# The first radial layer of two neighbouring edge groups on two row groups of PE, issued behind each other

## The chip, the cores and the metric

The kernel runs on one NeuronCore of a Trainium2 chip. The metric is the device time of one execution in microseconds (us), as the median of several runs.

## What is computed

A layer of a graph network: 6250 nodes with 160 channels (64 scalars and 32 vectors of three), 206250 edges sorted by their destination node.

```python
h = jnp.maximum(_layernorm(x, axis=-1), 0.0)
# per node: l0, l1 = linear maps of h times node_attr (the table that is gathered); si0, si1 likewise
h = jax.nn.relu(edge_length_embedded @ W_fc1 * (1.0 / np.sqrt(N_BASIS))) * RELU_GAIN   # 10 -> 100 per edge
w = h @ W_fc2 * (1.0 / np.sqrt(N_RADIAL))                                             # 100 -> 192 per edge
y0 = l0[edge_src]
y1 = l1[edge_src]
m0 = w0 * y0 * e0
m1 = (w1 * y0)[:, :, None] * e1[:, None, :]
m2 = (w2 * e0)[:, :, None] * y1
m3 = w3 * jnp.einsum('eud,ed->eu', y1, e1) * INV_SQRT3
s0 = jax.ops.segment_sum(m0, edge_dst, num_segments=N) * inv    # and s1, s2, s3
out = x + si + 0.5 * (the sums through four last linear maps)
```

## The kernel before

**The node stage.** The first part normalizes the nodes, applies the linear map and stores the result as a table in HBM. It ends before the first gather of the edge phase, and the change leaves it as it is.

**The edge phase.** The edges are taken in tiles of 128, four tiles (T) to a group, four groups (G) to a turn. A pair is two turns, that is 8 groups. There are 403 groups that hold edges. For each group:

- SP loads, once for two groups (HALF), the 10 radial numbers of each edge (`rad`), the source indices (`idx`) and the edge attributes (`attr_sb`), line 272, 277 and 281, into one of two buffers c. SP's queue is in order, and the three loads of a half wait for `fc1_done`, for `gathered` and for `msg_done`.
- GpSimd (POOL) issues four indirect DMAs (L357), each of which gathers 128 rows of the table into `y`. `y` has four slots, so the gathers of group g wait for the messages (`msg_done`) of group g - 4. There are 1612 of them, and GpSimd does nothing else in this phase.
- TensorE (PE) does the first radial layer `fc1` (L867: w_fc1 against `rad`, a contraction over 10 rows, 512 columns) into the bank s = g % 2 of `ps_h`.
- ScalarE (ACT) takes the relu of it into `hr` (L462).
- PE does the second layer `fc2` (L874, four products of 192 columns) into `ps_w`.
- VectorE (DVE) builds the one-hot matrices `hot` (L672, L679) and the dot products (L645, L649), multiplies `ps_w` with `y` into `msg` (L655, L660, L665), and adds the sums of the group before to `acc` (L707).
- PE sums the messages by node: `windows` (L902 with 128 columns and L904 with 64, four tiles each).

PE's instructions are in the order in which they are written out. In every step it does `fc1(g)`, `fc2(g - 1)`, `windows(g - 2)`. Every 8 groups the loop also finishes one block of 128 nodes: ACT normalizes it, PE turns it (`turn_block`, L880 and L881, into bank 1 of `ps_h`), ACT copies it (`move_block`, L467 and L468, which raises `hidt_done`), and PE ends it with six products (`last_linear`, L886 to L892). There are 47 such blocks in the loop. A further path, `general`, serves inputs whose edges are not sorted and doesn't run here.

## Time and profile before

| what | value |
|---|---|
| time, median of 3 runs | 2146.74 us (2144.57 to 2149.59) |
| span of the one profiled execution, which is its own time | 2932.2 us |
| PE busy in it | 2451.9 us (84%) |
| PE weight loads busy | 1929.8 us (66%) |
| DVE busy | 1690.4 us (58%) |
| ACT busy | 367.2 us (13%) |
| POOL busy | 1620.7 us (55%) |
| mean granted clock of PE | 0.776 of full speed |

### The profile page before, as it was taken

The page shows a single profiled execution, that of the slowest core. Times are in us where ns is not written, and L with a number is a line of the kernel's source. Part 1 is how long each engine was busy: PE and PEld are TensorE (multiplying, and loading weights), DVE is VectorE, ACT ScalarE, POOL GpSimd, SP SyncE. Part 2 cuts the span into 40 slices and gives each one's busy share as a digit, 9 for nine tenths or more (in the row PEclk, how much of TensorE's full clock was granted, in tenths as well). Part 3 has the DMA queues.
Part 4 walks back from the last instruction along what each step waited for, and adds up shares of the span by engine and source line. Part 5 has one row for each costly group of instructions (what it writes and reads, how often), then busy time and mean ns, then how long its engine had stood idle before and what let it go on. Part 6 is the DMA issues. An engine that isn't in the chain of part 4 may idle for free.

```text
span 2932.2 us, 42148 instructions
## 1 busy us (share of the span) xinstructions
PE 2451.9 (84%) x11361; PEld 1929.8 (66%) x11361; DVE 1690.4 (58%) x4677; ACT 367.2 (13%) x818; POOL 1620.7 (55%) x1629
## 2 busy tenths in 40 slices
PE   4688878888888888888889888888888888788988
PEld 3566666676666766666667666666676666676766
DVE  7355656555555655655655655555555556565655
ACT  4200101111111110111111111111111011111111
POOL 3455555555555656555555555555655555655653
PEclk9677877776877877887876878777878778778777
DMA  3222222222222222222222222122222222222222
GB/s 106 66 49 52 53 51 50 50 53 48 53 47 51 55 49 55 50 51 53 51 72 53 53 51 52 47 49 51 55 47 54 49 49 53 54 53 51 56 51 66
DMA packets 159836, 158.31 MB, mean 54 GB/s; under 512 B 86658, under 2 KB 131750, under 8 KB 159818
## 3 DMA queue, kind: packets, MB, share of 16 engines
q0 software_dynamic: 77376, 132.16, 18.3%
q1 hardware_dynamic: 81400, 24.49, 3.7%
q10 hardware_dynamic: 1042, 1.46, 0.2%
q8 instruction: 7, 0.11, 0.0%
q14 instruction: 11, 0.09, 0.0%
HBM read 149.94 MB, written 8.03 MB: 54 GB/s over the span
## 4 chain that ended last, share of the span: by engine, by line
PE 56%; another core or an unknown queue 16%; DVE 12%; issue 10%; DVEq 3%; ACT 1%; DMA 0%; ACTq 0%; SPq 0%
PE ps_w L874 17%; PE ps_s L902 13%; PE ps_h L867 11%; PE ps_s L904 11%; DVE hot L679 2%; DVE acc L707 2%; DVEq L710 2%; DVE dot L649 2%; DVE dots L645 2%; DVE hot L672 1%; DVE msg L665 1%; PE ps_s L890 1%; PE ps_s L891 1%; PE ps_s L886 1%
## 5 line engine op out<-in xcount | busy, mean ns | idle before, releaser
L357 POOL DMA_INDIRECT y<-table,idx x1612 | 1592.2, 988 | 1283.1 <-DVE msg L665 682.1
L874 PEld LDWEIGHTS ps_w<-w_fc,hr 100*128 100x128 f32 x3224 | 662.8, 235 | 464.2 <-issue 396.3
L874 PE MATMUL ps_w<-w_fc,hr 100*128 100x192 f32 x3224 | 814.9, 407 | 61.5 <-ACT hr L462 40.9
L707 DVE TENSOR_TENSOR acc<-acc,ps_s 64x32 f32 (+1 forms) x1612 | 327.3, 203 | 759.2 <-remote 480.6
L902 PE MATMUL ps_s<-hot,msg 128*128 128x128 f32 x3224 | 590.4, 336 | 95.1 <-issue 43.1
L902 PEld LDWEIGHTS ps_s<-hot,msg 128*128 128x128 f32 x3224 | 546.8, 245 | 140.0 <-DVE msg L665 62.4
L867 PE MATMUL ps_h<-rad,w_fc 10*100 10x512 f32 x806 | 547.7, 763 | 104.7 <-ACT hid_z L468 77.4
L904 PE MATMUL ps_s<-hot,msg 128*128 128x64 f32 x3224 | 512.3, 304 | 117.0 <-issue 116.5
L904 PEld LDWEIGHTS ps_s<-hot,msg 128*128 128x128 f32 x3224 | 499.0, 230 | 120.8 <-issue 119.8
L462 ACT ACTIVATE hr<-ps_h 100x512 f32<-100x512 f32 x403 | 238.7, 597 | 2433.7 <-remote 1026.9
L655 DVE TENSOR_TENSOR msg<-ps_w,y 128x512 f32<-128x512 f32 x403 | 278.7, 692 | 316.1 <-remote 172.3
L679 DVE TENSOR_TENSOR hot<-hot,attr_sb 128x512 f32<-128x512 f32 x403 | 276.0, 685 | 0.0
L649 DVE TENSOR_REDUCE dot<-dots 128x128 f32<-128x384 f32 x403 | 236.0, 586 | 0.0
L645 DVE TENSOR_TENSOR dots<-y,attr_sb 128x384 f32<-128x384 f32 x403 | 222.4, 552 | 9.6 <-DMA y<-table,idx 9.6
L660 DVE TENSOR_TENSOR msg<-ps_w,y 128x384 f32<-128x384 f32 x403 | 220.7, 548 | 0.0
L867 PEld LDWEIGHTS ps_h<-rad,w_fc 10*100 10x100 f32 x806 | 117.6, 186 | 151.1 <-ACT hid_z L468 82.8
L672 DVE TENSOR_TENSOR hot<-iota_w,dst_rel 128x128 f32<-128x128 f32 x403 | 118.1, 293 | 20.4 <-DMA attr_sb<-in_attr 5.1
L665 DVE TENSOR_TENSOR msg<-ps_w,dot 128x128 f32<-128x128 f32 x403 | 113.3, 281 | 0.0
L692 DVE SCALAR_TENSOR_TENSOR xres<-ps_s,a_sb,xres 128x160 f32 x47 | 17.8, 378 | 106.4 <-remote 77.9
L822 PE MATMUL ps_w<-wl,hid_t 128*128 128x128 f32 x98 | 30.4, 409 | 21.2 <-DVE y L546 20.7
L418 ACT ACTIVATE hid<-xres,shift,rstd 128x128 f32 (+1 forms) x98 | 47.6, 486 | 3.6 <-DVE shift L539 3.5
L886 PE MATMUL ps_s<-w_out,fin_in 128*128 128x160 f32 x94 | 27.0, 374 | 23.3 <-DVE msg L665 16.6
(83 smaller groups left out, 556.0 us busy)
## 6 DMA issues: line engine op xcount, KB each, us to landing
y<-table,idx POOLq DMA_INDIRECT x1612
rad<-in_radial SPq DMA_DIRECT2D x202, 40.0 KB
xres<-in_x SPq DMA_DIRECT2D x7, 560.0 KB, 4.1
table<-y SPq DMA_DIRECT2D x6, 560.0 KB, 3.2
out<-xres SPq DMA_DIRECT2D x6, 560.0 KB
idx<-in_src SPq DMA_DIRECT2D x202, 4.0 KB
attr_sb<-in_attr SPq DMA_DIRECT2D x202, 16.0 KB
dst_i<-in_dst ACTq DMA_DIRECT2D x1, 808.0 KB, 6.1
```

The costliest lines, as they stand in the source:

```text
L357: nc.gpsimd.indirect_dma_start(out=y[:, j, t, :], out_offset=None, in_=table, in_offset=bass.IndirectOffsetOnAxis(ap=idx[:, j // HALF, col ...
L462: nc.scalar.activation(hr[:, s, :], ps_h[0:N_RADIAL, s, 0:GE], ACT.Relu, scale=K_RADIAL).then_inc(relu_done, 1)
L645: nc.vector.tensor_tensor(dots[:, :, :, :], vectors(j), attr_of(j, 1, 4).unsqueeze(3).to_broadcast([P, T, 3, MUL1]), ALU.mult).then_inc(do ...
L649: nc.vector.tensor_reduce(dot[:, :, :], dots[:, :, :, :].rearrange("p t d u -> p t u d"), AX.X, ALU.add).then_inc(dot_done, 1)
L655: nc.vector.tensor_tensor(msg[:, s, :, 0:2 * MUL0].rearrange("p t (k u) -> p t k u", k=2), ps_w[:, s, :, 0:2 * MUL0].rearrange("p t (k u) ...
L660: nc.vector.tensor_tensor(msg[:, s, :, 2 * MUL0:M - MUL1].rearrange("p t (d u) -> p t d u", d=3), ps_w[:, s, :, 2 * MUL0:NW - MUL1].unsque ...
L679: nc.vector.tensor_tensor(hot[:, s, :, 1:V, :], hot[:, s, :, 0:1, :].to_broadcast([P, T, 4, W]), attr_of(j, 0, 4).unsqueeze(3).to_broadcas ...
L707: nc.vector.tensor_tensor(to, to, p[rows, cols].rearrange("p (v n) -> p v n", n=W), ALU.add).then_inc(acc_done, 1)
L867: nc.tensor.matmul(ps_h[0:N_RADIAL, j % 2, 0:GE], w_fc1[:, :], rad[:, j // HALF, (j % HALF) * GE:(j % HALF + 1) * GE], start=True, stop=Tr ...
L874: ins = nc.tensor.matmul(ps_w[:, s, t, 0:NW], hr[:, s, t * P:(t + 1) * P], w_fc2[:, :], start=True, stop=True)
L902: nc.tensor.matmul(ps_s[:, s, 0:4 * W], msg[:, s, t, 0:P], hot[:, s, t, 1:V, :], start=(t == 0), stop=(t == T - 1))
L904: ins = nc.tensor.matmul(ps_s[:, s, 4 * W:6 * W], msg[:, s, t, P:M], hot[:, s, t, 0:2, :], start=(t == 0), stop=(t == T - 1))
```

## The change

`w_fc1` and `rad` are laid out twice on partitions: the first group of a half on partitions 0 to 9, the second on partitions 32 to 41 (ROW = 32). `fc1_both` issues the first layers of two neighbouring groups behind each other, one on each of the two row groups of PE, into the two banks of `ps_h`. Then PE does for the first of the two groups `windows(g - 2)` and `fc2(g)`, and for the second `windows(g - 1)` and `fc2(g + 1)`. SP issues two loads of `rad` where it issued one, each with half of the bytes. ACT issues one more load of `w_fc1` at the start. The block's `turn_block` comes after the fc2 of the fourth group of a pair, `move_block` on ACT moves one relu later, and the wait for `hidt_done` stands ahead of the next `fc1_both`. At the end PE computes the first layer of one group that holds no edges, so that 404 first layers are issued instead of 403.

```diff
--- before.py
+++ after.py
@@ -27,6 +27,7 @@
 V = 5
 G = 4
 HALF = 2
+ROW = 32
 TURNS = -(-E // (P * T * G))
 GROUPS = TURNS * G
 TILES = GROUPS * T
@@ -90,7 +91,7 @@
         wlz = sb("wlz", [P, P])
         wself = sb("wself", [P, P])
         wselfz = sb("wselfz", [MUL1, MUL1])
-        w_fc1 = sb("w_fc1", [N_BASIS, N_RADIAL])
+        w_fc1 = sb("w_fc1", [ROW + N_BASIS, N_RADIAL])
         w_fc2 = sb("w_fc2", [N_RADIAL, NW])
         w_out = sb("w_out", [P, 4, C])
         stats = sb("stats", [P, CHUNK, 6])
@@ -106,7 +107,7 @@
         hid_z = sb("hid_z", [P, 2, P])
         idx = sb("idx", [P, 2, HALF * T], I32)
         attr_sb = sb("attr_sb", [P, 2, HALF * T, 4])
-        rad = sb("rad", [N_BASIS, 2, HALF * GE])
+        rad = sb("rad", [ROW + N_BASIS, 2, GE])
         y = sb("y", [P, G, T, C])
         hr = sb("hr", [N_RADIAL, 2, GE])
         msg = sb("msg", [P, 2, T, M])
@@ -269,7 +270,8 @@
                 if not first:
                     sp.wait_ge(fc1_done, (k - 1) * HALF)
                     sp.sem_inc(sp_passed, 1)
-                sp.dma_start(rad[:, c, :], radial[:, bass.ds(k * HALF * GE, HALF * GE)]).then_inc(ld_rad[c], 16)
+                for h in range(HALF):
+                    sp.dma_start(rad[h * ROW:h * ROW + N_BASIS, c, :], radial[:, bass.ds((k * HALF + h) * GE, GE)]).then_inc(ld_rad[c], 16)
                 if not first:
                     for j in range(HALF * c, HALF * c + HALF):
                         sp.wait_ge(gathered[j], i * (16 * T))
@@ -403,7 +405,8 @@
             act.dma_start(wself[:, :], w_self).then_inc(ld_w, 16)
             act.dma_start(wselfz[:, :], w_self_z).then_inc(ld_w, 16)
             act.dma_start(w_out[:, :, :], w_last).then_inc(ld_w, 16)
-            act.dma_start(w_fc1[:, :], wf1).then_inc(ld_w, 16)
+            for h in range(HALF):
+                act.dma_start(w_fc1[h * ROW:h * ROW + N_BASIS, :], wf1).then_inc(ld_w, 16)
             act.dma_start(w_fc2[:, :], wf2).then_inc(ld_w, 16)
             act.wait_ge(consts, 3)
@@ -477,9 +480,8 @@
                         relu(k * (2 * G) + j, j % 2, first and j < 2)
                         if finish and j == 1:
                             normalize(k - LAG, 0)
-                        if finish and j == 2:
+                        if finish and j == 3:
                             move_block(k - LAG, 0, 1)
-                        if finish and j == 3:
                             act.wait_ge(acc_done, k * (8 * G))
                             copy_block(k - LAG)
@@ -860,12 +862,12 @@
             ins.then_inc(flag_sum, 1)
             pe.wait_ge(w_scaled, 9)
 
-            def fc1(i, j):
-
-                if j % HALF == 0:
-                    pe.wait_ge(ld_rad[j // HALF], i * 16 + 16)
-                nc.tensor.matmul(ps_h[0:N_RADIAL, j % 2, 0:GE], w_fc1[:, :], rad[:, j // HALF, (j % HALF) * GE:(j % HALF + 1) * GE],
-                                 start=True, stop=True).then_inc(fc1_done, 1)
+            def fc1_both(i, c):
+
+                pe.wait_ge(ld_rad[c], i * (16 * HALF) + 16 * HALF)
+                for h in range(HALF):
+                    at = slice(h * ROW, h * ROW + N_BASIS)
+                    nc.tensor.matmul(ps_h[0:N_RADIAL, h, 0:GE], w_fc1[at, :], rad[at, c, :], start=True, stop=True).then_inc(fc1_done, 1)
 
             def fc2(g, s):
@@ -911,44 +913,46 @@
 
             def windowed():
                 def pair(k, first, finish):
-                    for j in range(2 * G):
+                    for j in range(0, 2 * G, HALF):
                         g = k * (2 * G) + j
-                        if finish and j == 3:
+                        if finish and j == 4:
                             pe.wait_ge(hidt_done, k - LAG + (BLOCKS + 1))
-                        fc1(k * 2 + j // G, j % G)
-                        if first and j == 1:
+                        fc1_both(k * 2 + j // G, j % G // HALF)
+                        if first and j == 0:
                             node_stage_left()
-                        if j >= 1 or not first:
-                            fc2(g - 1, (j - 1) % 2)
+                        for h in range(HALF):
+                            if j or not first:
+                                windows(g - HALF + h, h, first and j == HALF, k - LAG if finish and j == 6 and h == 1 else None)
+                            fc2(g + h, h)
                         if finish and j == 2:
                             turn_block(k - LAG, 0, 1)
-                        if j >= 2 or not first:
-                            windows(g - 2, j % 2, first and j < 4, k - LAG if finish and j == 7 else None)
 
                 pair(0, True, False)
                 with pe.Fori(1, LAG) as k:
                     pair(k, False, False)
                 with pe.Fori(LAG, PAIRS) as k:
                     pair(k, False, True)
-                for j in range(LEFT):
-                    g = (TURNS - 1) * G + j
-                    fc1(TURNS - 1, j)
-                    fc2(g - 1, (g - 1) % 2)
-                    windows(g - 2, g % 2, False)
                 last = EDGE_GROUPS - 1
-                fc2(last, last % 2)
+                assert LEFT == HALF + 1
+                fc1_both(TURNS - 1, 0)
+                for h in range(HALF):
+                    windows(last - 4 + h, h, False)
+                    fc2(last - 2 + h, h)
+                fc1_both(TURNS - 1, 1)
+                windows(last - 2, 0, False)
+                fc2(last, 0)
                 for n, b in enumerate(range(IN_LOOP, BLOCKS)):
                     turn_block(b, n, n)
-                windows(last - 1, (last - 1) % 2, False)
+                windows(last - 1, 1, False)
                 last_linear(IN_LOOP, 0, last_products(IN_LOOP))
-                windows(last, last % 2, False)
+                windows(last, 0, False)
                 last_linear(IN_LOOP + 1, 1, last_products(IN_LOOP + 1))
```

The first place is PE's rhythm and the turned block in the loop over pairs (rows as the program issues them; `ps_h<-rad,w_fc1` is a first layer, `ps_w<-w_fc2,hr` a second layer, `ps_s<-hot,msg` the sums; in square brackets the semaphores waited for). Before:

```order
L867 MATMUL ps_h<-rad,w_fc1 100x512 [waits ld_rad1]
L872 REGISTER_ALU
L874 MATMUL ps_w<-w_fc2,hr 128x192 [waits relu_done]
L874 MATMUL ps_w<-w_fc2,hr 128x192 x3
L879 REGISTER_ALU
L880 MATMUL ps_h<-ident,hid 128x128 [waits hid_done]
L881 MATMUL ps_h<-ident,hid_zs 32x128
L896 ISA
L902 MATMUL ps_s<-hot,msg 128x128 [waits acc_done,msg_done]
L902 MATMUL ps_s<-hot,msg 128x128 x3
L904 MATMUL ps_s<-hot,msg 128x64 x4
L867 MATMUL ps_h<-rad,w_fc1 100x512 [waits hidt_done]
```

Before, a group's sums stand between the turn of the block and the first layer that waits for ACT's copy of it. The same engine after the change, first the two first layers with what follows them:

```order
L870 MATMUL ps_h<-rad,w_fc1 100x512 [waits ld_rad1]
L870 MATMUL ps_h<-rad,w_fc1 100x512
L898 ISA
L904 MATMUL ps_s<-hot,msg 128x128 [waits acc_done,msg_done]
L904 MATMUL ps_s<-hot,msg 128x128 x3
L906 MATMUL ps_s<-hot,msg 128x64 x4
L874 REGISTER_ALU
L876 MATMUL ps_w<-w_fc2,hr 128x192 [waits relu_done]
L876 MATMUL ps_w<-w_fc2,hr 128x192 x3
```

The two first layers have come together ahead of a group's sums. Sums and second layers alternate as before; fc1 of the even group has gone behind a second layer, and that of the odd group has come forward past the sums. Further down on the same engine, at the turned block after the change:

```order
L876 MATMUL ps_w<-w_fc2,hr 128x192 x3
L881 REGISTER_ALU
L882 MATMUL ps_h<-ident,hid 128x128 [waits hid_done]
L883 MATMUL ps_h<-ident,hid_zs 32x128
L867 ISA [waits hidt_done]
L870 MATMUL ps_h<-rad,w_fc1 100x512 [waits ld_rad0]
L870 MATMUL ps_h<-rad,w_fc1 100x512
```

The sums that stood between the turn and the wait have moved away: the wait for `hidt_done` follows the turn directly.

## Rows read from the trace of the kernel before

**Rows 1.** The cores view of the whole run: span and mean granted clock.
```profile
core 0: 2932.2 us, clock 0.776
```

**Rows 2.** The page's chain that ended last, shares of the span by engine.
```profile
PE 56%; another core or an unknown queue 16%; DVE 12%; issue 10%; DVEq 3%; ACT 1%; DMA 0%; ACTq 0%; SPq 0%
```

**Rows 3.** The page's costliest groups: the gathers and the first-layer matmuls.
```profile
L357 POOL DMA_INDIRECT y<-table,idx x1612 | 1592.2, 988 | 1283.1 <-DVE msg L665 682.1
...
L867 PE MATMUL ps_h<-rad,w_fc 10*100 10x512 f32 x806 | 547.7, 763 | 104.7 <-ACT hid_z L468 77.4
```

**Rows 4.** The timeline from 94 us, GpSimd's first gathers and DVE's first use.
```profile
95.65 1.15 POOL L357 DMA_INDIRECT y<-table,idx  x1 [61.78 <-DMA idx<-in_src]
...
98.35 0.95 POOL L357 DMA_INDIRECT y<-table,idx  x1 [0.30 <-issue]
...
99.61 0.94 POOL L357 DMA_INDIRECT y<-table,idx  x1 [0.30 <-issue]
...
102.23 0.56 DVE L645 TENSOR_TENSOR dots<-y,attr_sb 128x384 f32<-128x384 f32 x1 [5.97 <-DMA y<-table,idx]
```

**Rows 5.** The timeline, GpSimd's last gather.
```profile
2908.24 0.95 POOL L357 DMA_INDIRECT y<-table,idx  x1 [0.30 <-issue]
```

**Rows 6.** The chain of waits: what GpSimd's gathers waited for, over the run.
```profile
POOL y L357 <- DVE msg L665: 682.1, 139, 7.9
```

**Rows 7.** The timeline of 117 us, PE slow with GpSimd at its pace.
```profile
116.23 0.95 POOL L357 DMA_INDIRECT y<-table,idx  x1 [0.30 <-issue]
...
117.05 0.26 PE L904 MATMUL ps_s<-hot,msg 128*128 128x64 f32 x1 [1.14 <-issue]
117.48 0.95 POOL L357 DMA_INDIRECT y<-table,idx  x1 [0.30 <-issue]
...
118.44 1.01 PE L867 MATMUL ps_h<-rad,w_fc 10*100 10x512 f32 x1 [1.13 <-issue]
```

**Rows 8.** The timeline of PE, one group at half clock, one at full.
```profile
1558.04 2.02 PE L867 MATMUL ps_h<-rad,w_fc 10*100 10x512 f32 x2
...
1565.99 1.10 PE L867 MATMUL ps_h<-rad,w_fc 10*100 10x512 f32 x2
1567.01 1.57 PE L874 MATMUL ps_w<-w_fc,hr 100*128 100x192 f32 x8
...
1570.53 1.10 PE L867 MATMUL ps_h<-rad,w_fc 10*100 10x512 f32 x2
```

**Rows 9.** Busy time by window over those groups, with the granted clock (PEclk).
```profile
1558.00:1565.70 7.70, 7.70 (x26) 6.11 (x25) 1.51 (x7) 0.28 (x1) 3.78 (x4) 0.50 0.21 53
1565.90:1570.50 4.60, 4.58 (x28) 3.40 (x27) 4.45 (x13) 1.40 (x4) 0.94 (x1) 1.00 0.02 4
```

**Rows 10.** The timeline of PE, the last product of a node block.
```profile
2921.61 0.49 PE L886 MATMUL ps_w<-w_out,fin_in 128*128 128x160 f32 x2
...
2923.25 1.16 PE L902 MATMUL ps_s<-hot,msg 128*128 128x128 f32 x8
```

**Rows 11.** The timeline of DVE, two groups behind each other.
```profile
1531.26 0.29 DVE L672 TENSOR_TENSOR hot<-iota_w,dst_rel 128x128 f32<-128x128 f32 x1
...
1535.36 0.29 DVE L672 TENSOR_TENSOR hot<-iota_w,dst_rel 128x128 f32<-128x128 f32 x1
```

**Rows 12.** The timeline of the turned block: PE's second transpose, ACT's second copy.
```profile
2918.13 0.27 PE L881 MATMUL ps_h<-ident,hid_zs 128*32 128x128 f32 x1
...
2918.61 0.25 ACT L468 ACTIVATE hid_z<-ps_h 32x128 f32<-32x128 f32 x1
```

**Rows 13.** The timeline of SP's queue, its first loads of the edge phase.
```profile
93.23 0.39 SPq L272 DMA_DIRECT2D rad<-in_radial  x1
93.67 0.37 SPq L277 DMA_DIRECT2D idx<-in_src  x1
```

**Rows 14.** Busy time by window, where PE stopped and the clock fell.
```profile
1436.00:1443.00 7.00, 2.31 (x10) 1.83 (x9) 0.00 (x0) 0.00 (x0) 4.97 (x6) 0.75 0.26 62
1443.00:1453.00 10.00, 9.52 (x31) 7.57 (x32) 7.84 (x22) 1.19 (x2) 2.54 (x3) 0.50 0.08 21
```

6 lines of the change are left out of this document (3 added, 3 removed).

## The prediction

> **What bounds the kernel now.** I read the cores view first. The profiled execution took 2932.2 us, which is its own time, at a mean clock of 0.776 [rows 1]. The median of the runs is 2146.74 us, 27% less. The trace therefore holds 785 us that a timed run doesn't have, and a share read off the page can't be carried over. The chain that ended last names PE with 56% [rows 2], and taken at its word it would promise that a cheaper PE pays. So the next question is which engine can't go faster than the timed run, whatever the profile adds.
>
> That is GpSimd. Its first gather starts at 95.65, and the third and the fourth at 98.35 and 99.61, 1.26 us apart: 0.95 us for the gather and 0.30 us until the next [rows 4]. Its last one starts at 2908.24 [rows 5], 23.96 us before the end. All 1612 at this pace make 95.65 + 1611 x 1.25 + 23.96 = 2133.4 us. Worked backwards, the median gives (2146.74 - 95.65 - 23.96) / 1611 = 1.258 us for a gather, against 1.25 to 1.26 in the rows. The page's mean of one is 988 ns [rows 3], which with 0.30 would be 1.29 and 2198 us, more than the median, so a timed run has fewer long gathers than the profile. In the profile GpSimd waited 682.1 us in 139 places for the messages of DVE [rows 6]: there the other engines were late, and a timed run can hold almost nothing of it, since 2146.74 - 2133.4 leaves 13 us for everything.
>
> Why is the profile slower? Around 117 us PE does single matmuls with 1.1 us of "issue" before each, while GpSimd keeps 1.25 us from gather to gather in the same microseconds [rows 7]. Such stops hit PE, not GpSimd. I take them for something of the profiled execution. That can't be shown from one trace, but the sum above speaks for it.
>
> Now the engines against GpSimd's 4 x 1.25 = 5.00 us for a group. PE at full clock goes from one first layer to the next in 1570.53 - 1565.99 = 4.54 us, and at half clock in 1565.99 - 1558.04 = 7.95 [rows 8, 9]. A node block adds 2923.25 - 2921.61 = 1.64 us of products per 8 groups, 0.2 per group [rows 10]. PE needs thus at most 4.7 us at full clock and 8.3 at half. DVE needs 1535.36 - 1531.26 = 4.10 [rows 11]. Both are below 5.00, PE by only 6%.
>
> **The change, part by part.**
>
> The two first layers side by side. Before, one takes 1567.01 - 1565.99 = 1.02 us at full clock until the second layer starts [rows 8], so 2.04 for two. The trace has no two matmuls on different row groups. The least that the pair can save is nothing (one after the other as now), the most is one whole first layer, 1.02 us, 0.51 per group. I take the middle, 0.25, since each matmul is two instructions of which only the last of the one and the first of the other are neighbours in the queue. The Trainium skill's page "TensorE: Matmul & The Clock Gate", section "Part 3: Packing small matmuls — row/col tiling", says that matmuls on distinct row groups run together and start some ns apart. By it the saving would be the upper end. Neither changes the sum, only how far PE stays under GpSimd. PE's group goes from 4.7 to between 4.2 and 4.7, and the time saved ends in PE's wait for messages. GpSimd is not touched by it: 0 us.
>
> The order on PE. Sums and second layers alternate as before: windows(g - 2), fc2(g), windows(g - 1), fc2(g + 1). Only the first layers move: fc1(g) goes behind fc2(g - 1), and fc1(g + 1) comes forward past windows(g - 2). The relu of g, which fc2(g) waits for, was covered by a second layer and the sums; now it is covered by fc1(g + 1) and the sums. `ps_w` and `hr` come free at the same points, so no wait is new here. The gathers are the queue that could suffer: those of group g + 4 need msg(g). From the start of the fourth gather of a group (99.61), DVE has the data at 102.23 [rows 4], and a whole DVE group is 4.10 [rows 11], so messages can be there 6.7 us after it. The gathers that need this slot are due 1.25 + 3 x 5.00 = 16.3 us after it. The margin is 9.6 us. The new order costs nothing as long as PE is late by less: 0 us.
>
> The turned block. ACT's second copy ends at 2918.61 + 0.25 = 2918.86, and the second transpose started at 2918.13 [rows 12], so PE stands some 0.7 us where before a group's sums covered that. 47 x 0.7 = 33 us of PE, 0.08 per group, under GpSimd's 5.00: 0 us; with that cover gone it would cost the 33 us.
>
> Loads. SP issues one more `rad` load before the first `idx`, which starts 93.67 - 93.23 = 0.44 us after it [rows 13]. The first gather waits for that `idx`: +0.44 us, once. In the loop SP's extra issue stands ahead of an `idx` that isn't needed for two groups (10 us): 0. ACT's extra load at the start is at most as much again: 0 to +0.44. The additional first layer at the end lies beside the last gathers: 0.
>
> Sum: 2146.74 + 0.44 + up to 0.44 = 2147.4 us. **Forecast 2147 us, no change.**
>
> **The rivals.**
>
> *PE bounds the timed run too.* Then 5.03 us per group, (2146.74 - 95.65 - 23.96) / 403, would be PE's, a mixture of 4.7 and 8.3. For it: PE's 56% [rows 2]. Against it: GpSimd's own pace gives the median within 0.6% with nothing fitted, and a PE that is never idle should have no reason to be at half clock (the clock fell after a stretch with PE busy 2.31 of 7.00 us [rows 14]). It would need gathers that are quicker untraced. It gives, with 0.25 saved at full clock, some 0.28 at this mixture, less 0.08: 403 x 0.20 = 81 us, so 2066; with the whole 0.51, 2147 - 403 x 0.49 = 1950. Chance 0.11.
>
> *Some of the 13 us above GpSimd's floor are waits for late messages*, and a PE with more room removes them: 2134 to 2142. Chance 0.09.
>
> *The clock goes down, and the kernel is slower.* With PE at 4.2 to 4.7 of 5.00 us there are more pauses, and a clock that falls in them makes a group 8.3 less 0 to 1.0. While it is down PE falls behind by about 1 - 5.00 / 7.8 = 0.36 us per us, so a stretch of 9.6 / 0.36 = 27 us at half clock uses up the margin; taken over the run, it decides when more than about a seventh of the groups are at half clock: 0.86 x 4.45 + 0.14 x 7.8 + 0.08 = 5.00. At a fifth it would be 5.20, 403 x 0.20 = +81 us, so 2228. For it: the fall after the pause [rows 14]. The Trainium skill's page "TensorE: Matmul & The Clock Gate", section "HAM oscillation — how this bites in real kernels", describes this for a matmul kernel that waits for its data, and the trace agrees that a pause precedes the fall. Against it: a PE that is behind has no pauses, and after 10 us of 9.52 busy at half clock [rows 14] the work goes on; and the room for it is larger than now. Chance 0.06.
>
> *The change doesn't do what it says* (the two matmuls don't overlap): PE stays at 4.7 + 0.08, still under 5.00, 2147. This lies within the forecast.
>
> **How the numbers follow.** Forecast and its variants 0.72, of which some 0.02 end beyond 0.2% on either side; small waits removed 0.09; PE-bound 0.11; clock 0.06; the rest, 0.02, is slower for a reason that I don't see. Within 0.2% (2142.4 to 2151.0): 0.70. Faster: 0.11 + 0.09 = 0.20. Slower: 0.06 + 0.02 + 0.02 = 0.10. 0.2%, 4.3 us, is about what a measurement of this kernel tells from no change. The range 2134 to 2156 begins at GpSimd's floor and leaves out the PE-bound and the clock rivals, 0.17.
>
> **What would show it.** In the changed profile GpSimd still goes 1.25 us from gather to gather inside a group, and the first gather starts at 96.1 instead of 95.65. Two first layers take between 1.02 and 2.04 us at full clock; PE waits longer for DVE's `msg`; fc1 waits for ACT's copy after the turn, 47 times 0.7 us. PE, which is late in the profiled execution, lets its span fall, by 403 x 0.2 = 80 us or more, while the median stays. The prediction is wrong if the median falls below 2134: then a timed gather is shorter than 1.25 us, and the bound was PE. It is wrong the other way if it rises by more than 9 us, with gathers that wait for `msg` in a timed run.

## The result, and the profile after

The changed kernel takes 2170.36 us (median of 4 runs, 2164.77 to 2175.91), the kernel before 2147.89 (4 runs, 2144.57 to 2149.59). The ratio is 1.0100, with a 95% interval of 1.0084 to 1.0115. That is slower by 1%, and outside the range of 2134 to 2156 that was forecast. The ratios of this document are formed from the comparable runs of each kernel, and can differ by some tenths of a per cent from the quotient of two medians.

The trace shown ahead of the prediction can't be laid beside the one of after. It looks like the traces from the chip of the first set of experiments, on which the kernel before takes 2892 to 2957 us in every run, with a profile or without (2933.97 in one whose span is 2932.2 as well). Below, "before" is therefore the profile of the first run of the second set, *before_2*, which took 2155.41 us.

The cores view and the page of after, the chain and two of its groups (which answer to [rows 1 to 3]):

```profile
core 0: 2167.2 us, clock 0.867
```

```profile
PE 29%; POOL 23%; issue 20%; DVE 14%; DMA 12%; DVEq 2%; ACT 1%; POOLq 0%; ACTq 0%; SPq 0%
...
L359 POOL DMA_INDIRECT y<-table,idx x1612 | 1558.4, 967 | 552.9 <-issue 455.9
...
L870 PE MATMUL ps_h<-rad,w_fc 10*100 10x512 f32 x808 | 249.8, 697 | 33.5 <-ACT hid_z L471 28.5
```

The chain of waits of after: who waited, for whom, us in total, how often, the longest.

```profile
POOL y L359 <- issue: 455.9, 1497, 0.3
...
DVE dots L647 <- DMA y<-table,idx: 202.1, 246, 6.0
...
PE ps_s L904 <- DVE msg L667: 117.1, 117, 2.4
...
PE ps_s L888 <- DVE msg L667: 39.9, 27, 4.4
...
POOL y L359 <- DVE msg L657: 33.2, 109, 0.3
PE ps_h L870 <- ACT hid_z L471: 28.5, 47, 0.6
```

The same of before, from *before_2*: the cores view,

```profile
core 0: 2153.6 us, clock 0.933
```

its page,

```profile
L357 POOL DMA_INDIRECT y<-table,idx x1612 | 1551.1, 962 | 553.2 <-issue 446.4
```

and its chain of waits.

```profile
POOL y L357 <- issue: 446.4, 1464, 0.3
...
DVE dots L645 <- DMA y<-table,idx: 269.5, 324, 6.0
...
PE ps_s L902 <- DVE msg L665: 59.0, 120, 1.5
...
PE ps_s L886 <- DVE msg L665: 15.6, 27, 1.0
```

The chain's shares (PE 29%, POOL 23%, issue 20%) name no single bound, so the waits have to be read. They say four things. Once it has its first indices, GpSimd waits for nobody: its longest wait for a message is 0.3 us, which is the gap that it has after every gather. Its idle time is the same, 552.9 against 553.2. But the gathers themselves are longer, 1558.4 us against 1551.1, with the same 1612 instructions. And DVE, which in before stood waiting for its gather in 324 of 403 groups, does so in 246: it comes late more often. PE, for its part, waits more for messages (157 us against 75, the two `msg` rows of each added), and its clock is lower.

Where do gathers get longer? The timeline of after, GpSimd and DVE's product of `hot` and the attributes (L681), three groups:

```profile
1504.16 0.69 DVE L681 TENSOR_TENSOR hot<-hot,attr_sb 128x512 f32<-128x512 f32 x1
1504.56 1.11 POOL L359 DMA_INDIRECT y<-table,idx  x1 [0.30 <-issue]
...
1508.37 0.69 DVE L681 TENSOR_TENSOR hot<-hot,attr_sb 128x512 f32<-128x512 f32 x1
1508.47 1.40 POOL L359 DMA_INDIRECT y<-table,idx  x1 [0.30 <-issue]
...
1513.31 0.69 DVE L681 TENSOR_TENSOR hot<-hot,attr_sb 128x512 f32<-128x512 f32 x1
...
1513.93 0.95 POOL L359 DMA_INDIRECT y<-table,idx  x1 [0.30 <-issue]
```

A gather that starts 0.10 us after this product takes 1.40 us, one that starts 0.40 us after it 1.11, and one at 0.62 the plain 0.95. In the third group DVE had waited for its gather (0.76 us before its dot products). After such a wait the next gather starts 0.5 to 0.8 us behind the product's start in 240 of 246 groups. A DVE that is late has no such tie to GpSimd, and its product drifts across the starts of gathers.

Counted over the whole trace, this is where the lengthening sits. In the groups in which DVE had waited, the gathers that start beside its first products (L647 and L681) take 1.4 us more in all than 0.945 us each. In the 157 groups in which it was late they take 31.8 us more. In *before_2* it is 2.0 us in 324 groups and 21.3 us in the 79 late ones.

Why is DVE late? The timeline of PE in after, at a node block, and the windows over it (the columns as in [rows 9]):

```profile
1471.56 1.52 PE L876 MATMUL ps_w<-w_fc,hr 100*128 100x192 f32 x8
1474.81 0.53 PE L888 MATMUL ps_s<-w_out,fin_in 128*128 128x160 f32 x2 [1.73 <-DVE msg L667]
...
1480.91 2.87 PE L876 MATMUL ps_w<-w_fc,hr 100*128 100x192 f32 x8
```

```profile
1470.00:1475.00 5.00, 3.27 (x25) 2.98 (x25) 4.02 (x12) 0.21 (x1) 3.78 (x4) 1.00 0.28 66
1475.00:1480.00 5.00, 5.00 (x24) 4.71 (x24) 3.74 (x10) 0.00 (x0) 3.78 (x4) 0.53 0.32 77
1480.00:1485.00 5.00, 5.00 (x18) 3.68 (x17) 3.53 (x10) 0.00 (x0) 3.78 (x4) 0.50 0.28 66
```

PE stands 1.73 us for a message, the granted clock goes from 1.00 (2.4 GHz) to 0.50 (1.2 GHz) behind it, and the second layer that took 1.52 us takes 2.87. PE falls behind, and with it DVE. This is no single case: of the 32 falls of the clock in the edge phase of after, 30 come shortly behind a pause of PE of over 1 us. But not every such pause is followed by a fall (there are 69 of them), and *before_2* has 21 falls there, of which only one comes after such a pause.

### The profile page after: what moved, and what is told of

It is laid out like the page before. It is cut to its first block, busy times and chain, and to the rows that moved or that the text cites. A ratio compares the mean times of both kernels' runs of the same rounds, so it can differ in the third digit from the quotient of the medians.

```text
span 2167.2 us, 42755 instructions
## 1 busy us (share of the span) xinstructions
PE 1925.7 (89%) x11363; PEld 1633.5 (75%) x11363; DVE 1704.5 (79%) x4677; ACT 348.8 (16%) x818; POOL 1586.9 (73%) x1629
## 4 chain that ended last, share of the span: by engine, by line
PE 29%; POOL 23%; issue 20%; DVE 14%; DMA 12%; DVEq 2%; ACT 1%; POOLq 0%; ACTq 0%; SPq 0%
POOL y L359 23%; DMA y<-table,idx 11%; PE ps_w L876 8%; PE ps_s L904 8%; PE ps_s L906 6%; DVE hot L681 4%; PE ps_h L870 3%; DVE msg L657 3%; DVE dot L651 3%; DVEq L712 1%; DVE dst_rel L629 1%; DVE dots L647 1%; DVE acc L709 1%; DVE msg L667 1%; PE ps_s L892 0%
## 5 line engine op out<-in xcount | busy, mean ns | idle before, releaser
L359 POOL DMA_INDIRECT y<-table,idx x1612 | 1558.4, 967 | 552.9 <-issue 455.9
L904 PEld LDWEIGHTS ps_s<-hot,msg 128*128 128x128 f32 x3224 | 461.5, 218 | 324.9 <-DVE msg L667 200.5
L876 PE MATMUL ps_w<-w_fc,hr 100*128 100x192 f32 x3224 | 701.5, 367 | 0.8 <-ACT hr L465 0.8
L904 PE MATMUL ps_s<-hot,msg 128*128 128x128 f32 x3224 | 530.4, 315 | 117.4 <-DVE msg L667 117.1
L876 PEld LDWEIGHTS ps_w<-w_fc,hr 100*128 100x128 f32 x3224 | 594.2, 214 | 2.4 <-issue 2.4
L906 PE MATMUL ps_s<-hot,msg 128*128 128x64 f32 x3224 | 462.2, 293 | 0.0
L906 PEld LDWEIGHTS ps_s<-hot,msg 128*128 128x128 f32 x3224 | 454.3, 217 | 0.0
L465 ACT ACTIVATE hr<-ps_h 100x512 f32<-100x512 f32 x403 | 218.8, 594 | 1403.1 <-PE ps_h L870 1403.1
L647 DVE TENSOR_TENSOR dots<-y,attr_sb 128x384 f32<-128x384 f32 x403 | 224.6, 557 | 202.7 <-DMA y<-table,idx 202.1
L870 PE MATMUL ps_h<-rad,w_fc 10*100 10x512 f32 x808 | 249.8, 697 | 33.5 <-ACT hid_z L471 28.5
L681 DVE TENSOR_TENSOR hot<-hot,attr_sb 128x512 f32<-128x512 f32 x403 | 276.1, 685 | 0.0
L870 PEld LDWEIGHTS ps_h<-rad,w_fc 10*100 10x100 f32 x808 | 55.9, 174 | 87.6 <-issue 82.5
L470 ACT ACTIVATE hid_t<-ps_h 128x128 f32<-128x128 f32 x49 | 13.6, 278 | 360.9 <-PE ps_h L883 360.9
L888 PE MATMUL ps_s<-w_out,fin_in 128*128 128x160 f32 x94 | 26.5, 368 | 39.9 <-DVE msg L667 39.9
L888 PEld LDWEIGHTS ps_s<-w_out,fin_in 128*128 128x128 f32 x94 | 17.2, 215 | 48.4 <-issue 47.7
```

Of the source, the lines that this page charges most:

```text
L359: nc.gpsimd.indirect_dma_start(out=y[:, j, t, :], out_offset=None, in_=table, in_offset=bass.IndirectOffsetOnAxis(ap=idx[:, j // HALF, col ...
L465: nc.scalar.activation(hr[:, s, :], ps_h[0:N_RADIAL, s, 0:GE], ACT.Relu, scale=K_RADIAL).then_inc(relu_done, 1)
L647: nc.vector.tensor_tensor(dots[:, :, :, :], vectors(j), attr_of(j, 1, 4).unsqueeze(3).to_broadcast([P, T, 3, MUL1]), ALU.mult).then_inc(do ...
L681: nc.vector.tensor_tensor(hot[:, s, :, 1:V, :], hot[:, s, :, 0:1, :].to_broadcast([P, T, 4, W]), attr_of(j, 0, 4).unsqueeze(3).to_broadcas ...
L870: nc.tensor.matmul(ps_h[0:N_RADIAL, h, 0:GE], w_fc1[at, :], rad[at, c, :], start=True, stop=True).then_inc(fc1_done, 1)
L876: ins = nc.tensor.matmul(ps_w[:, s, t, 0:NW], hr[:, s, t * P:(t + 1) * P], w_fc2[:, :], start=True, stop=True)
```

## The experiments

The theories at the start were those of the prediction: GpSimd bounds the kernel and something lengthens its path (a wait, a load), or PE has become the bound. The theory of the long gathers came out of the profile after. All ratios are to the kernel before on the same chip.

### First set, on a chip like that of the first profile

*before_again* is the unchanged kernel.

> The kernel before, unchanged, for a second profile. Theory 1 (a gather of GpSimd takes 0.1 to 0.45 us longer when it starts while DVE multiplies two SBUF operands, L679 or L645, and the change altered how often that happens): a profile of about 2147 us in which GpSimd never waits, with gathers above 1.0 us that sum to 10 to 15 us over the 945 ns of a plain one, against 34 us in the changed kernel. Theory 2 (the extra loads of rad slow GpSimd): about as many long gathers as the number of loads explains, evenly spread. Theory 3 (PE is late more often after the change): here too GpSimd has waits for msg, in the changed kernel more of them.

It took 2933.97 us, and the other 17 runs of the unchanged kernel there have a median of 2921.22. The runs without a profile are as slow as those with one. So the slowness, and very likely the stops of PE in [rows 7] with it, belongs to the chip and not to the profiled execution, as I had taken it.

*rad_split* is before, with `rad` loaded by two DMAs per half:

```diff
-sp.dma_start(rad[:, c, :], radial[:, bass.ds(k * HALF * GE, HALF * GE)]).then_inc(ld_rad[c], 16)
+for h in range(HALF):
+    sp.dma_start(rad[:, c, h * GE:(h + 1) * GE], radial[:, bass.ds((k * HALF + h) * GE, GE)]).then_inc(ld_rad[c], 16)
```

> The kernel before with only its rad loads split in two (404 issues of 20 KB in place of 202 of 40 KB), everything else as before. Theory 1: within 0.3% of 2147 us, unless the shift of SP moves DVE, which it should not. Theory 2 (the loads are the cause): 2165 to 2175 us. Theory 3: 2147 us.

2925.22 us, ratio 0.9999 (0.9948 to 1.0050): the additional loads cost nothing that shows. As GpSimd waits for messages on this chip (below), this is no test of what they cost where it doesn't. There the traces answer: from the first gather to the end of the last, all that isn't a gather is 490.7 us in after and 491.2 in *before_2*.

*same_rows* is after with both first layers on partitions 0 to 9, so that they can't run together; the order on PE is that of after.

```diff
-at = slice(h * ROW, h * ROW + N_BASIS)
-nc.tensor.matmul(ps_h[0:N_RADIAL, h, 0:GE], w_fc1[at, :], rad[at, c, :], ...)
+nc.tensor.matmul(ps_h[0:N_RADIAL, h, 0:GE], w_fc1[:, :], rad[:, c, h, :], ...)
```

> The changed kernel with its order of instructions and its loads, but both first layers on the same row group of PE, so that they cannot run beside each other. Theory 1: PE is slower than in the changed kernel by up to 1 us per pair, DVE is later behind the gathers, and the sum of the long gathers changes; anything from 2140 to 2190 us, with the time above 2134 us equal to the sum of the long gathers within 5 us. Theory 2: as the changed kernel, 2170 us. Theory 3: slower than the changed kernel, 2175 us or more.

2978.46 us, ratio 1.0222 (1.0165 to 1.0279).

*hot_first* is before with the product of `hot` and attributes moved ahead of the wait for the gather:

```diff
+dve.wait_ge(hot_done, g + 1)
+nc.vector.tensor_tensor(hot[:, s, :, 1:V, :], hot[:, s, :, 0:1, :]..., attr_of(j, 0, 4)..., ALU.mult)
 dve.wait_ge(gathered[j], i * (16 * T) + 16 * T)
 edge_dots(j)
-dve.wait_ge(hot_done, g + 1)
-nc.vector.tensor_tensor(hot[:, s, :, 1:V, :], ...)
```

> The kernel before with one DVE instruction moved: the product of hot with the attributes (L679, 0.6 us) runs ahead of the wait for the gather, instead of behind the dots. No engine has more work. Theory 1: where DVE waits for the gathers, the product now starts 0.03 to 0.15 us before the first gather of each group, so that this gather takes about 1.35 us instead of 0.945; up to 403 x 0.4 = 160 us more, 2230 to 2310 us. Theories 2 and 3: 2147 us, as no load is added and PE has less to wait for.

3001.59 us, ratio 1.0302 (1.0212 to 1.0392). On this chip GpSimd waits for messages for 515 to 729 us in the four profiles, so a DVE or PE that is later costs directly, and nothing about a kernel bound by GpSimd can be read from it. The second set repeats *same_rows* and *hot_first*.

### Second set: is it the product?

*before_2* is the unchanged kernel, for its profile.

> The kernel before, for a profile on a chip where it takes 2147 us. Theory 1 (a gather is longer when it starts while DVE reads two SBUF operands): GpSimd never waits for a message, and the gathers above 1.0 us sum to 10 to 15 us over 945 ns each, against 34 us in the changed kernel. Theory 3 (PE late after the change): GpSimd has some waits for msg in both.

2155.41 us, with the rows above. The 18 other runs of the kernel before on this chip have a median of 2158.06, to which the ratios of this set refer. The gathers hold 27.8 us over 1612 plain ones of 0.945 us, where 10 to 15 were expected.

*hot_psum_after* is after, with the first part of `hot` copied to PSUM by DVE and read there by the product, which stands behind the scalar products (only the lines of the new place are shown):

```diff
+nc.vector.tensor_copy(ps_w[:, s, :, NW:NW + W], hot[:, s, :, 0, :]).then_inc(hot_out, 1)
 scalar_products(j, s)
+dve.wait_ge(hot_out, g + 1)
+nc.vector.tensor_tensor(hot[:, s, :, 1:V, :], ps_w[:, s, :, NW:NW + W]..., attr_of(j, 0, 4)..., ALU.mult)
```

> The changed kernel, in which DVE's product of hot and the attributes reads hot from PSUM instead of SBUF (one more DVE copy of 128 x 128 into free columns of ps_w, and the product stands behind the scalar products). PE, ACT, SP and GpSimd have the same instructions, DVE has 0.2 to 0.3 us more per group. Theory 1: only the dots (L647) are left to collide, the long gathers sum to 5 to 15 us, and the time falls to 2140 to 2152 us, 1% below the changed kernel. Theory 3: the same as the changed kernel or slower, 2170 us or more, since DVE has more work.

2147.68 us, ratio 0.9954 (0.9938 to 0.9970), in the range expected and faster than the kernel before, though DVE has an instruction more in each group.

*hot_first_2* is *hot_first* again.

> The kernel before with the product of hot and the attributes ahead of the wait for the gather, once more, where the kernel before takes 2147 us. Theory 1: DVE waits for the gathers there, so that the product starts 0.03 to 0.15 us before a group's first gather in most groups: +80 to +160 us, 2230 to 2310 us. Theory 3: 2147 us.

2142.39 us, ratio 0.9932 (0.9912 to 0.9953): faster, where 80 us or more of loss were expected. My arithmetic of where the product would fall was wrong. The timeline of *hot_first_2*:

```profile
1509.96 0.95 POOL L357 DMA_INDIRECT y<-table,idx  x1 [0.30 <-issue]
1510.05 0.69 DVE L676 TENSOR_TENSOR hot<-hot,attr_sb 128x512 f32<-128x512 f32 x1
1511.21 0.94 POOL L357 DMA_INDIRECT y<-table,idx  x1 [0.30 <-issue]
```

The product starts 0.09 us behind the gather, lies beside nearly all of it, and the gather keeps 0.95. So it is not the overlap that counts but which of the two starts first. The gathers' busy time here is 1534.8 us, 16.3 us below *before_2*.

*same_rows_2* is *same_rows* again.

> The changed kernel's order and loads with both first layers on the same row group, once more, where the kernel before takes 2147 us. Theory 1: time above 2134 us equals the sum of the long gathers within 5 us, whatever it is. Theory 3: slower than the changed kernel, 2175 us or more, with GpSimd waiting for msg.

2500.17 us, ratio 1.1619 (1.1579 to 1.1659). The cores view and the chain of waits:

```profile
core 0: 2471.9 us, clock 0.755
```

```profile
POOL y L359 <- DVE msg L667: 253.1, 109, 5.0
...
DVE dots L647 <- DMA y<-table,idx: 27.6, 21, 5.9
```

Here GpSimd does wait: the margin of 9.6 us is used up, and DVE is ahead of its gather in 21 groups only. The rule that was expected, a time above 2134 us equal to the sum of the long gathers, doesn't hold any more. The clock is 0.755 (0.74 in the middle of the run, where PE is busy for 1579.42 of 1600 us). This shows how much the order on PE and the clock can cost, but it has two changes in one against after (no overlap, and ten rows of the array at work where a pair of after has twenty). *full_rows_same* in the fourth set keeps the first and takes back the second.

### Third set: one operand in SBUF or in PSUM

*after_2* is after again.

> The changed kernel, unchanged, on one chip with the other three and with the kernel before. Theory 1 (its time is GpSimd's gathers at 1.25 us each, plus the sum of those that were lengthened by DVE): 1.01 times the kernel before, with 30 to 40 us of lengthening in the profile against 22 us in that of the kernel before.

2164.48 us, ratio 1.0075 (1.0057 to 1.0094).

*timed_sbuf* and *timed_psum* are after with the copy and the product directly ahead of the scalar products. They have the same instructions in the same order, and differ in one operand (- is *timed_sbuf*, + is *timed_psum*, the lines without a sign are in both):

```diff
 nc.vector.tensor_copy(ps_w[:, s, :, NW:NW + W], hot[:, s, :, 0, :]).then_inc(hot_out, 1)
 dve.wait_ge(hot_out, g + 1)
-nc.vector.tensor_tensor(hot[:, s, :, 1:V, :], hot[:, s, :, 0:1, :].to_broadcast([P, T, 4, W]), ...
+nc.vector.tensor_tensor(hot[:, s, :, 1:V, :], ps_w[:, s, :, NW:NW + W].unsqueeze(2).to_broadcast([P, T, 4, W]), ...
```

> The changed kernel with DVE's product of hot and the attributes put behind the dot sums and one copy of 128 x 128 (the copy goes to PSUM and isn't read), so that it starts 0.1 to 0.2 us before a gather in the groups in which DVE waited for its data. Both operands of the product are in SBUF. Theory 1: a gather of nearly each group takes 1.2 to 1.35 us, so +80 to +120 us against the changed kernel, 2250 to 2300 us. Theory 3 (PE is late): DVE has 0.25 us more in a group and still needs less than GpSimd; within 5 us of timed_psum.

> The same instructions in the same order as timed_sbuf, but the product reads the copy in PSUM in place of hot in SBUF. Theory 1: few long gathers (those from the dots alone), 2140 to 2160 us, so 4 to 6% below timed_sbuf. Theory 3: the same time as timed_sbuf.

On this chip the kernel before has a median of 2147.19. With both inputs in SBUF the time is 2188.38 us, ratio 1.0187 (1.0160 to 1.0213); with one in PSUM 2144.73, ratio 0.9981 (0.9969 to 0.9993). The gathers' row on the page of *timed_sbuf*

```profile
L360 POOL DMA_INDIRECT y<-table,idx x1612 | 1578.9, 979 | 557.0 <-issue 451.3
```

and of *timed_psum*:

```profile
L360 POOL DMA_INDIRECT y<-table,idx x1612 | 1534.8, 952 | 553.1 <-issue 439.8
```

The times differ by 43.7 us, the gathers by 44.1. Of the gathers that start right behind the product, those of *timed_sbuf* hold 39.8 us over 0.945 us each, those of *timed_psum* less than 0.1. That DVE's product with both inputs in SBUF lengthens gathers, and that this is what the kernel pays, is shown by this pair. The size was not foreseen: *timed_sbuf* is 24 us slower than *after_2*, where 80 to 120 were expected, and 2.0% above *timed_psum* instead of 4 to 6%.

*hot_first_after* is the edit of *hot_first* on after.

> The changed kernel with the product of hot and the attributes ahead of the wait for the gather, as in hot_first, which took 0.993 of the kernel before with 10 us of lengthening. Theory 1: the product then falls where no gather starts in the groups in which DVE waits, but PE is late more often than in hot_first, so 15 to 25 us of lengthening stay: 2145 to 2160 us. Theory 3: as the changed kernel, 1.01 times the kernel before.

2148.95 us, ratio 1.0007 (0.9992 to 1.0021), with PE's order as in after and the clock still at 0.877. That is 15.5 us less than *after_2*, and the time of the kernel before. But the same edit made the kernel before faster too (*hot_first_2*, 0.9932), and between these two the gathers still differ by 8.2 us (1543.0 and 1534.8), about as much as between after and *before_2*. So moving the product pays in both kernels, and doesn't take away what the change costs. What a product that reads PSUM would leave of the change's loss was not tried on the kernel before.

### Fourth set: the clock

*full_rows_same* is *same_rows* with `rad` and `w_fc1` filled up to 128 partitions with zeros, which leaves the result as it is, and *full_rows_before* the same on before, whose lines are these:

```diff
-w_fc1 = sb("w_fc1", [N_BASIS, N_RADIAL])
+w_fc1 = sb("w_fc1", [P, N_RADIAL])
-rad = sb("rad", [N_BASIS, 2, HALF * GE])
+rad = sb("rad", [P, 2, HALF * GE])
+nc.gpsimd.memset(w_fc1[:, :], 0.0).then_inc(padded, 1)
+nc.gpsimd.memset(rad[:, :, :], 0.0).then_inc(padded, 1)
```

> same_rows (the changed order, both first layers behind each other on one row group, 1.16 times the kernel before) with the first layer's operands padded with zeros from 10 to 128 rows, so that its matmuls take as long and use all rows of PE. Theory 4 (PE's clock fell in same_rows because 2 us of matmuls on 10 rows stand together, although PE was busy): the clock rises from 0.755 to 0.9 or more and the time falls to 1.00 to 1.03 of the kernel before. Theory 5 (PE's order alone is too long for GpSimd's 5.00 us): the time stays near 1.16.

> The kernel before with the first layer padded with zeros to 128 rows, nothing else. Theory 4: the clock rises from 0.933 to 0.96 or more, fewer groups in which DVE is late, 10 to 15 us of lengthening in place of 22: 0.994 to 0.998 of the kernel before. Theory 5: no difference, 1.000.

*full_rows_same*: 2170.31 us, ratio 1.0092 (1.0072 to 1.0113), against 1.1619 without the zeros; its clock is 0.886, a little under the 0.9 expected. *full_rows_before*: 2135.73 us, ratio 0.9934 (0.9922 to 0.9947). That is faster than both kernels. Its cores view and its gathers, which hold 3.8 us over 1612 plain ones:

```profile
core 0: 2135.5 us, clock 0.984
```

```profile
L362 POOL DMA_INDIRECT y<-table,idx x1612 | 1527.1, 947 | 552.2 <-issue 446.0
```

*after_fill* is after with two of the second layer's four matmuls done twice:

```diff
-for t in range(T):
+for t in (0, 1, 0, 1, 2, 3):
```

> The changed kernel with two of the four products of each second layer done twice (same operands, same place), so that PE has 0.7 us more work in each group and fewer pauses. Theory 6 (the change is slower because PE's pauses let its clock fall, DVE is then late, and its product lengthens gathers): the clock rises from 0.875 to 0.92 or more, the late groups go from 153 towards 80 and the time to 1.000 to 1.004 of the kernel before, so work added to PE makes it faster. Theory 3 (PE's work is what is too long): slower than the changed kernel, 1.015 or more.

2152.75 us, ratio 1.0017 (1.0000 to 1.0033), clock 0.955, against 1.0075 for *after_2* and 1.0100 for after. More work for PE, in the same order, makes after faster by 0.6 to 0.8%, and takes back most of the change's loss. *full_rows_hot_first* joins *full_rows_before* and *hot_first*.

> The padded first layer together with the product of hot ahead of the wait for the gather (hot_first alone took 0.9932). Theories 1 and 4: under 5 us of lengthening, 0.990 to 0.992 of the kernel before, 2134 us being GpSimd's floor. Theory 5: 0.993, as hot_first alone.

2136.55 us, ratio 0.9947 (0.9934 to 0.9960), where 0.990 to 0.992 was expected: nothing is added to *full_rows_before*, whose gathers are already nearly plain.

### Fifth and sixth: which pause

*turn_covered* is after with the turned block one group of sums earlier, so that these cover ACT's copy:

```diff
-if finish and j == 2:
-    turn_block(k - LAG, 0, 1)
+    if finish and j == 2 and h == 0:
+        turn_block(k - LAG, 0, 0)
```

> The changed kernel with the turned block put between the second layer and the sums of the pair's first group (into the other bank of ps_h), so that ACT's copy of it is covered and PE no longer waits 0.6 us for it 47 times. Theory 6 (pauses of PE let the clock fall): the wait goes, the clock rises a little, 0.875 to about 0.89, and the time falls by 2 to 8 us, to 1.004 to 1.007 of the kernel before. If that wait is not one of the pauses that matter: 1.0075, as the changed kernel.

2177.66 us, ratio 1.0133 (1.0109 to 1.0156). The wait for ACT is gone, but the kernel is slower than after and its clock is lower, where a higher clock and 2 to 8 us less were expected.

```profile
core 0: 2179.6 us, clock 0.838
```

Its timeline of PE shows the wait at the next place:

```profile
1501.62 0.27 PE L883 MATMUL ps_h<-ident,hid_zs 128*32 128x128 f32 x1
1503.22 1.16 PE L904 MATMUL ps_s<-hot,msg 128*128 128x128 f32 x8 [1.33 <-DVE msg L667]
```

In place of the 0.6 us for ACT, PE waits 1.33 for the message. Over the run the clock goes down as often as in after (36 times and 37), but is down for 706 us in all instead of 576. Whether it is the longer pause that costs the clock was not tried on this kernel. On *full_rows_same* it could be, since there the clock falls at one place of the node block. Its timeline and windows:

```profile
1518.33 1.52 PE L881 MATMUL ps_w<-w_fc,hr 100*128 100x192 f32 x8
1521.40 0.90 PE L893 MATMUL ps_s<-w_out,fin_in 128*128 128x160 f32 x2 [1.55 <-DVE msg L673]
...
1527.97 2.87 PE L881 MATMUL ps_w<-w_fc,hr 100*128 100x192 f32 x8
```

```profile
1508.00:1516.00 8.00, 8.00 (x54) 6.88 (x53) 6.78 (x17) 1.25 (x3) 6.06 (x7) 1.00 0.31 69
...
1524.00:1530.00 6.00, 6.00 (x26) 5.94 (x26) 3.87 (x12) 0.00 (x0) 4.48 (x6) 0.50 0.29 66
```

*fill_at_block* fills just that pause, 47 times in the run, by doing the second layer ahead of it twice:

```diff
-for t in range(T):
+for t in ([0, 1, 2, 3] if again else []) + [0, 1, 2, 3]:
...
-fc2(g + h, h)
+fc2(g + h, h, finish and j == 6 and h == 0)
```

> full_rows_same with one thing more: in the group before a node block's products, 47 times in the run, the second layer is done twice (1.4 us of PE at full clock), which fills the 1.6 us for which PE stands before those products. In full_rows_same the clock is 1.00 until that pause and 0.50 for some 9 us after it, in 35 of the 47 blocks. Theory (the pause lets the clock fall, the fallen clock makes PE and DVE late, a late DVE has its product of hot and attributes at the starts of gathers, and these take longer): the clock goes from 0.886 to 0.97 or more, DVE waits for its gather in more than 330 groups instead of 224, the gathers' busy time falls from 1568.8 to at most 1540, and the time from 1.009 to between 0.993 and 1.000 of the kernel before, although PE has 65 us more to do. Rival 1 (the late DVE comes from the order on PE itself, not from the clock): the clock rises, the number of groups and the gathers' time stay, 1.007 to 1.011. Rival 2 (the clock falls at the next pause instead): clock 0.87 to 0.91 and 1.007 to 1.012. Rival 3 (a longer second layer makes DVE late in those groups): 1.012 or more, with the clock up.

2144.93 us (12 runs), ratio 0.9988 (0.9975 to 1.0001), against 1.0092 for *full_rows_same*. The cores view, the chain of waits and the gathers' row of the page of *fill_at_block*:

```profile
core 0: 2140.1 us, clock 0.959
```

```profile
DVE dots L653 <- DMA y<-table,idx: 288.1, 363, 6.0
...
PE ps_s L893 <- DVE msg L673: 14.0, 33, 0.6
```

```profile
L364 POOL DMA_INDIRECT y<-table,idx x1612 | 1535.2, 952 | 552.3 <-issue 450.8
```

and what *full_rows_same* has in the same two waits:

```profile
DVE dots L653 <- DMA y<-table,idx: 190.0, 224, 6.1
...
PE ps_s L893 <- DVE msg L673: 76.6, 46, 4.3
```

The pause goes, the clock rises from 0.886 to 0.959, DVE is ahead in 363 groups instead of 224, and the gathers lose 33.6 us (1568.8 to 1535.2). The groups, the gathers and the time are as expected; the clock stays a little under the 0.97 that was. The order on PE is untouched, so in this kernel it is not the order by itself that makes DVE late, but the pause that it leaves, through the clock. For after itself *after_fill* says the same, with less precision, since it adds work in every group. After has a second candidate that was not separated from the pauses: its pair of first layers keeps few rows of PE at work, and since the two operands lie side by side on the partitions, they can't be filled up to 128 rows.

### All profiles side by side

| kernel | own time of the profiled execution | gathers busy | difference | groups in which DVE waited for its gather | clock |
|---|---|---|---|---|---|
| full_rows_before | 2137.26 | 1527.1 | 610.2 | 390 | 0.984 |
| fill_at_block | 2141.84 | 1535.2 | 606.6 | 363 | 0.959 |
| before_2 | 2155.41 | 1551.1 | 604.3 | 324 | 0.933 |
| after_fill | 2161.93 | 1550.8 | 611.1 | 289 | 0.955 |
| after | 2168.99 | 1558.4 | 610.6 | 246 | 0.867 |
| after_2 | 2163.63 | 1560.8 | 602.8 | 244 | 0.875 |
| full_rows_same | 2172.95 | 1568.8 | 604.1 | 224 | 0.886 |
| turn_covered | 2181.37 | 1570.9 | 610.5 | 197 | 0.838 |
| same_rows_2 | 2473.61 | 1603.8 | 869.8 | 21 | 0.755 |
| *product moved or changed:* | | | | | |
| full_rows_hot_first | 2131.64 | 1528.0 | 603.6 | 369 | 0.983 |
| hot_first_2 | 2141.13 | 1534.8 | 606.3 | 265 | 0.933 |
| timed_psum | 2144.55 | 1534.8 | 609.8 | 181 | 0.885 |
| hot_first_after | 2148.84 | 1543.0 | 605.8 | 204 | 0.877 |
| hot_psum_after | 2155.86 | 1543.0 | 612.9 | 167 | 0.876 |
| timed_sbuf | 2189.94 | 1578.9 | 611.0 | 138 | 0.868 |

The difference is 603 to 613 us in all but *same_rows_2*, which has 253 us of real waits of GpSimd: but for a spread of 10 us, the time of this kernel is a constant plus what its gathers take. 1612 plain gathers of 0.945 us are 1523.3 us.

The spread of the constant is as large as the step from *before_2* to after, so it has to be looked at. It lies behind the last gather. The windows from the end of the last gather to the end of the kernel, in after and in *before_2*:

```profile
2145.43:2167.20 21.77, 16.27 (x67) 14.80 (x66) 7.99 (x25) 2.69 (x8) 0.00 (x0) 0.50 0.10 30
```

```profile
2138.58:2153.60 15.02, 8.05 (x58) 7.07 (x58) 8.75 (x27) 2.22 (x6) 0.00 (x1) 0.89 0.15 44
```

This last stretch belongs to PE and DVE, and takes 15.0 us at a clock of 0.89 and 21.8 at 0.50. It is not the change that makes it long: *after_2* has 14.9 us at 0.89, *full_rows_before* 22.1 at 0.50. All profiles but *same_rows_2* have 14.8 to 22.1. The clock isn't all of it, since *after_fill* has 21.9 us at 0.87. In the upper part, where the product is where the kernel has it, the gathers get longer by a step wherever DVE is ahead in fewer groups (one pair, 0.3 us apart, stands the other way). The lower part shows the rest: the same lateness costs less when the product starts elsewhere, and least when it reads PSUM (1534.8 us with 181 groups in *timed_psum*, where the upper part has 1570.9 with 197).

The untraced runs of one kernel say the same of the clock. Of 23 runs of the unchanged kernel in the third set, the one with the highest mean clock, 0.943, took 2140.58 us, and the one with the lowest, 0.924, took 2152.94. Over all 23 the time falls as the clock rises (correlation -0.78).

## Why the prediction was wrong

**"PE's group goes from 4.7 to between 4.2 and 4.7."** Right, and at the upper end of the saving. The timeline of PE in after:

```profile
1510.98 1.10 PE L870 MATMUL ps_h<-rad,w_fc 10*100 10x512 f32 x4
1512.02 1.16 PE L904 MATMUL ps_s<-hot,msg 128*128 128x128 f32 x8
```

A pair takes 1.04 us where two took 2.04 [rows 8], so the whole 0.5 per group is saved. By the Trainium skill's page "TensorE: Matmul & The Clock Gate", section "Part 3: Packing small matmuls — row/col tiling", it should be so, and the trace agrees.

**"GpSimd is not touched by it: 0 us."** This is the step that failed. No wait of GpSimd and none of its instructions changed, and I took the length of a gather for a constant. It depends on what DVE starts just before. The term that I put at nothing is 7.3 us between the profiles of *before_2* and after, and 9.7 with *after_2*. The page's mean of 988 ns against 0.95 us in the timeline [rows 3, 4] held this already: I wrote that "a timed run has fewer long gathers than the profile" and never asked what made them long. In the timeline shown, gathers and DVE's products stood some rows apart. The 13 us between the floor and the median, which I left to small waits, were such gathers, and they were more than 13. The floor itself was too high: its last term, 23.96 us from the start of the last gather to the end, came from the slow chip, and is 16.0 in *before_2*. The sum for that profile closes as 2133.4 + 0.6 (a later first gather) - 8.0 + 27.8 (1551.1 - 1523.3) = 2153.8, against a span of 2153.6. One run of *full_rows_before* took 2130.56 us, below the floor. The Trainium skill's "GPSIMD Engine Reference", section "Key points", says that GpSimd shares its SBUF interfaces with VectorE and contends with instructions that have two SBUF inputs. The pair *timed_sbuf* and *timed_psum* agrees, 1578.9 against 1534.8. Its page "SBUF — State Buffer", section "Who interferes with whom", reports an older probe in which such an instruction did not stall a DMA. Here it lengthens indirect DMAs of GpSimd, of which the longest takes 1.475 us in after instead of 0.945, and the measurement decides.

**"The new order costs nothing as long as PE is late by less" than 9.6 us.** This is the same error at its second place. Its premise held: GpSimd waits for no message. The sign that I had named for a rise of more than 9 us, "gathers that wait for `msg` in a timed run", did not come; the time rose by 22 us without it. The conclusion fell, since lateness inside the margin has a price of its own, paid in gathers. The step also looked only at who waits for whom, and not at how long PE's pauses are. With the first layers in pairs, half of the groups have only a second layer between the sums of two neighbouring groups, and PE waits longer for the message there: 39.9 us ahead of the node block's products (38.5 in *after_2*), where before has 15.6.

**The clock rival** had the sign and the first half of the mechanism: more pauses, and a clock that falls from 0.933 to 0.867. I priced it only through waits of GpSimd, which made it an all-or-nothing case of 2228 us at 0.06. The real price is gradual, and starts at the first late group. Against the rival I wrote that a PE that is never idle should have no reason to be at half clock. *same_rows_2* shows the contrary: PE busy for 1579.42 of 1600 us at 0.74. The section "HAM oscillation — how this bites in real kernels" of the Trainium skill's page "TensorE: Matmul & The Clock Gate", cited in the prediction, describes a clock that falls after waits for data. The rows at 1474.81 agree with that; the falls of *same_rows_2*, where PE hardly waits, are of another kind.

**"The turned block ... 47 x 0.7."** The row has 47 waits of 0.6 us at most, 28.5 us together, where I had 33. Removing them (*turn_covered*) gave nothing back; they were no term of the loss as I had meant it.

**Loads.** The first gather of after starts at 96.41 us, that of *before_2* at 96.20, that of *after_2* at 95.5; the loop has no more time between its gathers than before (490.7 us against 491.2). Below 1 us, as in the sum.

**"I take them for something of the profiled execution"** was wrong: the runs without a profile are as slow (*before_again*). So the span that was to fall by 80 us or more in the profiled execution could not be looked at: the profile ahead of the prediction comes from a slow chip, that of after doesn't.

How far the sum closes. The spans of after and *before_2* differ by 13.6 us: 0.2 up to the first gather, 7.3 in the gathers, -0.6 between them, and 6.7 behind the last one, where the clock is 0.50 against 0.89; *after_2* doesn't have these 6.7. The span of *after_2* is 8.3 us longer than that of *before_2*, of which 9.7 in its gathers and the rest taken back elsewhere. The medians, however, differ by 17 to 22 us. *before_2* took 6 to 8 us more than the medians of the kernel before in the other sets (2147.19 to 2149.44; in its own it is 2158.06), so 7 to 10 us of gathers and these 6 to 8 give 13 to 18 of the 17 to 22; the rest isn't accounted for. That the untraced runs lose their time in the same way is inferred from the table, not seen. What also stays open is the exact reason for the clock of *turn_covered*, and of *same_rows_2*, where it is at 0.755 with PE hardly ever idle.

## What to carry to other kernels

An engine that issues gathers can be the bound without ever waiting, and its time can still depend on others: compare the busy time of one and the same instruction between two profiles before taking its duration as given, and ask of every long one what started just before it. Where a product of two SBUF operands on DVE can be placed so that it starts after a gather and not before the next, or can read one operand from PSUM, that is worth 15 to 20 us here (44 against the worst place tried), where all the time taken from PE was worth nothing. A PE that has less to do than the bound is not free: here the time saved gathered in pauses of over a microsecond, the clock fell behind many of them, and the saving was given back with interest. Filling the pauses won most of it back. And before the end of the last gather is taken for the end of the kernel, look at what follows it: here it is 15 to 22 us, from one execution to another.
